# A graph network kernel: the first node group's window loads wait for one stored edge group, and the last layer's first edge groups go through transposes and products one at a time

## What is computed

```python
def conv(h, i):
    msg = h[src] * edge_weight[:, None]
    agg = segment_sum(msg, dst, num_segments=N)
    return agg @ W_rel[i] + b_rel[i] + h @ W_root[i]
h = relu(conv(x, 0)); h = relu(conv(h, 1)); h = conv(h, 2)
x = layernorm(x + h)
...
for g in range(3):                       # group = edge_type // 10
    msg = msg + (group == g) * (x[src] @ W[g] + b[g])
out = segment_sum(msg, dst) / max(deg, 1)
x = layernorm(x + relu(out))
```

## Time and profile before

| | |
|---|---|
| Median of three executions | 1523.29 us (1519.26 to 1525.98) |
| The profiled execution | 1535.58 us, of which the span of the trace is 1533.8 us |
| TensorE busy | 1231.4 us, 80% of the span |
| VectorE busy | 1000.4 us, 65% |
| ScalarE busy | 729.7 us, 48% |
| GpSimd busy | 839.9 us, 55% |
| Mean granted TensorE clock | 0.929 of full speed |

### The profile page before, as it was taken

The page is one execution under the profiler, slowest core; times in us unless marked ns, Lnnn a source line. Parts: engine busy times, 40 slices in busy tenths (PEclk is TensorE's granted clock), DMA queues, the critical chain, the costliest instruction groups (busy, mean ns, idle before and its releaser), DMA issues.

```text
span 1533.8 us, 36546 instructions
## 1 busy us (share of the span) xinstructions
PE 1231.4 (80%) x6476; PEld 874.4 (57%) x6476; DVE 1000.4 (65%) x4006; ACT 729.7 (48%) x1674; POOL 839.9 (55%) x1154
## 2 busy tenths in 40 slices
PE   0599999999489997888387776777489999999984
PEld 0488888777368776666255454555335545554553
DVE  5566666555336554444188886777618999978887
ACT  0144443222134441222077775667615777666666
POOL 4766665551377775550676664552065666655620
PEclk9899999999789999999699998889859999989995
DMA  2599999999568889999499998999525666678885
GB/s 63 142 287 299 303 304 309 347 357 342 202 218 271 257 257 330 364 358 349 156 301 312 298 302 301 328 349 343 188 79 158 204 207 209 206 230 268 265 250 199
DMA packets 293061, 403.05 MB, mean 263 GB/s; under 512 B 43478, under 2 KB 202839, under 8 KB 292970
## 3 DMA queue, kind: packets, MB, share of 16 engines
q10 hardware_dynamic: 87120, 266.66, 47.2%
q1 hardware_dynamic: 180538, 83.67, 20.5%
q0 software_dynamic: 25312, 51.78, 12.9%
HBM read 222.77 MB, written 179.16 MB: 262 GB/s over the span
## 4 chain that ended last, share of the span: by engine, by line
DMA 26%; PE 24%; DVE 14%; issue 14%; SPq 11%; ACT 5%; POOL 3%; ACTq 2%; DVEq 2%; POOLq 0%
DMA resid<-in_x 8%; PE ps_node L1252 6%; DMA win<-edge_rows 6%; PE ps_node L1243 6%; PE ps_pair L1275 5%; SPq L541 4%; DVE ln_stats L1030 4%; DMA feat_t<-spill 3%; SPq L544 3%; DMA edge_rows<-edge_out 3%; SPq L533 3%; POOL gather_ring L648 3%; DMA win<-plain_rows 3%; ACT rows L1462 2%; PE ps_pair L1220 2%
## 5 line engine op out<-in xcount | busy, mean ns | idle before, releaser
L648 POOL DMA_INDIRECT gather_ring<-h,src_ring x588 | 566.3, 963 | 275.9 <-issue 146.3
L1252 PEld LDWEIGHTS ps_node<-place,win 128*128 128x128 f32 x1764 | 289.8, 196 | 225.1 <-issue 169.9
L1252 PE MATMUL ps_node<-place,win 128*128 128x171 f32 (+1 forms) x1764 | 320.2, 318 | 60.8 <-DMA win<-plain_rows 50.0
L1408 ACT ACTIVATE next_t<-ps_node,rel_bt 128x512 f32<-128x512 f32 x294 | 199.8, 680 | 251.8 <-PE ps_node L1252 242.4
L971 DVE TENSOR_SCALAR place<-iota_row,window_node,window_weight 128x171 f32<-128x171 f32 (+1 forms) x882 | 279.3, 372 | 0.2
L1010 DVE COPY rows<-ps_pair 128x512 f32<-128x512 f32 x196 | 135.3, 690 | 213.7 <-PE ps_pair L1275 209.7
L1243 PE MATMUL ps_node<-feat_t,root_w 128*128 128x512 f32 x380 | 206.6, 627 | 49.3 <-DMA feat_t<-spill 46.0
L1462 ACT ACTIVATE rows<-pre,ln_shift,ln_rstd 128x128 f32<-128x128 f32 x576 | 235.5, 481 | 16.1 <-issue 10.9
L648 POOL DMA_INDIRECT gather_ring<-in_x,src_ring x196 | 186.9, 954 | 71.5 <-issue 53.0
L1275 PE MATMUL ps_pair<-rel_w,next_t 128*128 128x128 f32 x1568 | 209.4, 277 | 3.7 <-ACT next_t L1408 3.7
L1275 PEld LDWEIGHTS ps_pair<-rel_w,next_t 128*128 128x128 f32 x1568 | 199.2, 193 | 4.6 <-ACT next_t L1408 4.5
(11 more groups left out here) (115 smaller groups left out, 1157.2 us busy)
## 6 DMA issues: line engine op xcount, KB each, us to landing
h<-rows ACTq DMA_DIRECT2D x121, 512.0 KB
win<-plain_rows SPq DMA_DIRECT2D x588, 64.0 KB
edge_rows<-edge_out ACTq DMA_DIRECT2D x98, 264.0 KB
feat_t<-in_x_t ACTq DMA_DIRECT2D x49, 512.0 KB
plain_rows<-gather_ring ACTq DMA_DIRECT2D x98, 256.0 KB
resid<-in_x ACTq DMA_DIRECT2D x49, 512.0 KB
out_x<-rows ACTq DMA_DIRECT2D x49, 512.0 KB
spill<-next_t ACTq DMA_DIRECT2D x46, 512.0 KB
```

The costliest lines, as they stand in the source:

```text
L648: pool.indirect_dma_start(out=gather_ring[:, k.slot(4), j, 0:D], out_offset=None, in_=h_tabs[l][:, :], in_offset=bass.IndirectOffsetOnAxis ...
L1252: op = pe.matmul(bank[:, lo:hi], rows_j[:, 0:D], place_j, start=False, stop=(j == kind.count - 1))
L1408: act.activation(next_t[:, g.slot(4), :], ps_node[b][:, :], func, bias=rel_bt[:, l:l + 1]).then_inc(s_next, 1)
```

## The change

Three places change. SP loads the first node group's windows once edge group 0 is stored, and only then waits for edge group 1. `pace` gets 512 for the first node group, which takes one drain and one small memset on VectorE. TensorE's lead changes in layer 3: for k from 0 to 3 it does the transposes of group k and then the products of group k, and the transposes of group 4 after all of them. In layer 0 TensorE's order stays; layers 1 and 2 have no edge work on TensorE. ScalarE's and VectorE's lists stay.

```diff
-                    for k in ([m] if isinstance(m.n, int) and m.n == 0 else []) + [m.plus(1)]:
+                    def stored(k):
                         if not k.outside(EDGE_GROUPS):
                             sp.wait_ge(s_edge_st[k.slot(4)], 16 * (k.uses(4, EDGE_GROUPS, l) + 1))
                             sp.sem_inc(s_idle, 1)
+                    very_first = isinstance(m.n, int) and m.n == 0
+                    stored(m if very_first else m.plus(1))
                     load_windows(l, first_group(m))
+                    if very_first:
+                        stored(m.plus(1))
                     load_windows(l, first_group(m).plus(1))
...
             dve.tensor_copy(pace[:, :], pace_i[:, :])
+            dve.drain()
+            dve.memset(pace[0:1, :], float(GD))
             dve.wait_ge(s_pre, 1)
...
                     edges_here = not passes_edges(l)
-                    if edges_here:
+
+                    if l == 0:
                         edge_transposes(l, At(0, 0, BODY))
                     for k in range(LEAD if edges_here else 0):
-                        edge_transposes(l, At(0, k + 1, BODY))
+                        edge_transposes(l, At(0, k + (l == 0), BODY))
                         for tiles in first_halves(l):
                             edge_products(l, At(0, k, BODY), tiles)
+                    if l == LAYERS:
+                        edge_transposes(l, At(0, LEAD, BODY))
```

## The result

The changed kernel took 1537.39 us (median of 20 executions, 1528.38 to 1552.69), the kernel before 1529.68 us (median of 20, 1516.11 to 1545.55). The ratio is 1.007, with a 95% interval from 1.0046 to 1.0094: slower by 7 to 14 us. The three executions of before that stood at the prediction had a median of 1523.29, 6.4 us under that of all 20.

The account below looks back on a forecast made before the run. It took ScalarE's gathers and stores to bound the starts of layers 1 and 2, and TensorE's lead at 1.2 GHz layer 3's. Terms 0 + 0 + 0 + 5.3 us on 1523.29 gave 1528.5 us, range 1518 to 1535.5.

Parts of the forecast that it names:

- The SP edit and `pace` at nothing: Layers 0 to 2: earlier window loads and the `pace` operations taken at 0 us, with -3.55 us twice kept for the range.
- the same order: Layer 2: `features` of group 0 taken to stand behind the lead's stores as in layer 1, so no gain.
- The order of the lead at 1.2 GHz: Layer 3's lead: products start 4.43 us earlier, but gaps of 1.27 us leave group 3 0.3 us later, 0.6 at most.
- The walk: Layer 3's lead, group by group at 1.2 GHz: group 3 starts at 1147.19 us, where it started at 1146.92.
- The sentence behind the walk: Layer 3's lead: 4.43 us and group 4's transposes, 1.04 us, are eaten by three gaps and four exposed loads.
- The clock decides the rest: End of layer 3's lead: loss between +0.6 us, clock rising as before, and 5.26 us, rising only with the first node groups.
- 2.65 + 0.92 + 1.69 = 5.26: Layer 3: group 3 ends 2.65 us late, then the first node group and two tiles of products run at 1.2 GHz.
- case 3: Layer 3: clock low through the second node group too, or executions behind the median rose earlier; 8.7 us, 1532.0; chance 0.15.
- case 1: Layer 3: lead at 1.2 GHz, clock back with the first node groups; 1528.5 us, range 1524 to 1532; chance 0.48.
- The base: Whole kernel: the median of 1523.29 us for the kernel before, to which the sum of 5.3 us was added.
- The advice against idle gaps between bursts: Layer 3's lead: skill page advice cited as speaking against the edit; no size given.

Follow-up runs that it names:

- windows_only: The changed kernel with TensorE's layer 3 lead put back in the old order, leaving SP's waits and `pace` changed; ratio 1.0002 to the kernel before.
- lead_only: The kernel before with only TensorE's new order in layer 3's lead; ratio 1.0064 to the kernel before.
- after_third: The changed kernel, unaltered, in a third profile; clock at 0.50 up to 57 us, third node group at 62.2 us after layer 2's last store.
- fill: The changed kernel with one spare TensorE product behind the transposes of groups 1, 2 and 3 in layer 3's lead; ratio 0.9999 to the kernel before.
- hot_after: The changed kernel with 22 spare TensorE products ahead of layer 3's lead; ratio 0.9939 to the kernel before, though medians were 1535.06 against 1531.51 us.
- warm_halves: The changed kernel with the lead of `halves` and 16 spare TensorE products ahead of it; ratio 0.9973 to the kernel before.
- warm_after: The changed kernel with 16 spare TensorE products ahead of layer 3's lead; ratio 1.0055 to the kernel before.
- hot_halves: `warm_halves` with 22 spare products instead of 16; ratio to the kernel before 0.989, then 0.9973 when repeated with more rounds.
- warm_before: The kernel before with 16 spare TensorE products ahead of layer 3's lead; ratio 0.9995 to the kernel before.
- after_again: The changed kernel, unaltered, profiled once more; third node group at 56.9 us after layer 2's last store.
- after_fourth: The changed kernel, unaltered, in a fourth profile; clock up at 26 us, third node group at 52.0 us after layer 2's last store.
- halves: The kernel before with layer 3's next transposes put between two halves of a group's products, which start early; ratio 0.9988 to the kernel before.

## Why the prediction was wrong

**The SP edit and `pace` at nothing: right.** Loads and products came some 5 us earlier and `features` did not move. `windows_only` at 1.0002 shows it for all layers together. In layer 2 the row of before names TensorE's node products and not a store as what `features` waited for the earlier trace rows, so the prediction's "the same order" was not read from it; that `features` did not move there (26.50 and 26.63 us) bears it out.

**The order of the lead at 1.2 GHz: right, to half a us.** The early start was put at 4.43 us and was 4.40. The break was put at 1.27 us and was 1.29, with `scale_rows` as its releaser. The walk gives 10.34 us from transposes to transposes, measured 10.40, and group 3 started 0.53 us later where 0.3 was expected. The sentence behind the walk, by which the transposes of group 4 are a further gain of 1.04 us, does not fit it (5.47 us gained, 5.01 lost) and is not needed: in both orders three transposes stand between the first products and those of group 3.

**The step that failed is "The clock decides the rest", and the sum over it.** I took the lead of the one profiled execution for that of every execution. In it the clock rose at 45 us, in group 3, and the order of before gained only 2.08 us from that. That was the latest rise of the four traces of this order: the others rose at 19, 29 and 20 us, and their third node groups stand 3 to 10 us earlier, 5.4 us in the mean of all four. To lose a rise in group 0 or 1 costs more than to lose one in group 3. The term "2.65 + 0.92 + 1.69 = 5.26" against the profiled execution measured 7.9 against the mean of four (and 8.2 between the two profiled executions, where the clock stayed low through the second node group as well, as case 3 has it). Where the clock did come back with the first node groups, as case 1 has it, in `lead_only` and `after_third`, the third node group stood some 4.9 us behind the profiled lead of before, close to the 5.26: there the new order was sized well, and what it was compared with was not the usual lead of before. Case 3 names this very mechanism, that the executions behind the median rose earlier; I gave it 0.15, with nothing in the one trace to set it by. The spread of 6.7 us among three executions could have been a hint.

**The base was too low besides, and that is the larger part of the miss.** I moved the sum to a median of three, 1523.29; over 20 executions it is 1529.68. Of the 8.9 us between 1528.5 and 1537.39, 6.4 are the base and 2.5 the term: from 1529.68 the sum would have said 1534.9.

**The break as the cause of the low clock.** `lead_only` places the loss in the new order, and `fill`, which takes only the idleness away and keeps the period of 10.4 us, brings 1.007 back to 0.9999; the medians of these two were 1543.09 and 1532.59 us, against the same 1529.90. `hot_after` shows a full clock lost in that order in group 1, behind a break of 1.29 us. Of the kernels that differ in the order alone, `warm_halves` had a lost clock back after 6 us and `warm_after` after 44, `hot_halves` after 7 (twice) and `hot_after` after 24; single traces spread here too, as `warm_before`, without such breaks, took 27 us, and `after_again`, with them, 14. So it is shown that the order costs by its breaks, by the ratios first of all. It is not shown that the clock must stay low under it: `after_fourth` held it for 17 us. The order of before had the clock up at some point of the lead and kept it to the lead's end in four traces of four, that of the change in two of five (`after_fourth`, and `after_again` from 45 us on); the other three stayed low through the whole lead. What in the single execution decides between them stays open.

The Trainium skill, "TensorE: Matmul & The Clock Gate", Part 1, section "A second HAM failure mode: psum-queue depth-cycling", tells of a kernel in which short idle times between groups of matmuls make the clock go up and down. `after_again` (up at 29 us, down at 32, up at 45) shows the like. The advice against idle gaps between bursts, in the same page of the Trainium skill, section "Why this matters for your kernels", which the prediction set against the edit, is for gaps longer than these; here the clock stayed low in leads with one gap of 1.29 us to a group, and in the one trace with 0.69 us.

**What beats both.** The lead of `halves` with spare products ahead of it gave 0.9973 (`warm_halves`), 0.989 and 0.9973 (`hot_halves`, twice). The first and the last interval just touch 1, so a gain of some 0.3% is likely and not shown. The third node group came at 44.7 to 45.0 us in all three traces.

## What to carry to other kernels

To start a chain earlier by taking work out of its shadow is worth the start minus one exposed hand-over for every turn, and the hand-over holds all that stands ahead on the other engine's list, here a scaling behind a copy. Before TensorE work is reordered in a stretch at the low clock, count the idle breaks that the new order makes: here three of 1.29 us ate the early start and 0.53 us more as time, and the rest of the 7.9 us came through the clock. Where a clock's rise moves between executions, one profile is one draw of it; the stage has to be seen several times before a change of it is sized.

## What was not expected of the hardware

TensorE can be busy for 29.51 of 30 us and stay at 1.2 GHz, and a lead of the same order was at full clock 19 or 20 us after the last store in other executions. A spare product that fills an idle break cost nothing here and paid: `fill` issues three more products than the change and its ratio is 0.007 lower. The full clock that 16 spare products reached or kept was lost again behind waits of 2.79 to 5.24 us for a gather.
